# Making the mask rows of two attention layers on VectorE instead of ScalarE

## The chip, the cores and the metric

The kernel runs on one core of a Trainium2 chip. The metric is the device time of one execution, in microseconds (us). Three timed runs of the kernel before took 3186.9, 3188.81 and 3189.63 us; the median is 3188.81.

## What is computed

Eight layers work in turn on x, 128 sequences of 64 tokens with 128 features (8192 rows): four pairs of a gated cross-attention and a gated feed-forward layer. Every layer adds its result to x. The change touches the first and the last cross-attention, which have a mask over the context's 64 tokens. Cut to what matters, with scale = 64 ** -0.5:

```python
def L0_xattn(x, context, mask, W_q, W_k, W_v, W_o, b_o):   # 8 heads of 64, context 64 x 96
    q, k, v = x @ W_q, context @ W_k, context @ W_v
    sim = einsum('bhid,bhjd->bhij', q, k) * scale
    sim = where(mask[:, None, None, :], sim, max_neg)
    out = einsum('bhij,bhjd->bhid', softmax(sim), v)
    return out @ W_o + b_o

def L3_xattn(...):    # 16 heads of 64, one learned null key and value more, layer norms of x and of the result
    full_mask = pad(mask, ((0, 0), (1, 0)), constant_values=True)
    sim = where(full_mask[:, None, None, :], sim, max_neg)
```

## The kernel before

The whole of x stays on the chip as 64 tiles of 128 rows (two sequences each). The layers run one after another with a barrier between them. Each engine has its own program; order between engines comes from semaphores alone, and inside an engine from the order of its program.

`wide_attention` does the three wide cross-attentions. Layer 0 and layer 3 have `masked` set, the middle one not. The rows are worked in groups of four tiles (TG = 4, 16 groups). A `Unit` is one group and eight heads, so layer 0 has 16 units and layer 3, with 16 heads in two passes, has 32. A unit has four steps, t = 0 to 3, one tile each. The loop over units goes by twos (u = 0 and 1); its first and last passes are written out and the middle ones are a hardware loop. The counter n numbers the steps.

In step n TensorE transposes the probabilities of tile n (L777), projects the output of tile n - 1 (L709), multiplies probabilities and values (L699), makes the scores of tile n + 2 (L687), then the values of tile n + 1 and one key and one query product of a unit further on (L349 to L351). PSUM holds one set of scores (`ps_s`).

ScalarE copies results out of PSUM: the transposed probabilities (L916), the output (L925), values (L846), keys (L838) and queries (L842), and takes the exponential (`probs`, L863). GpSimd scales the probabilities (`scale_probs`, L561 and L562), splits and spreads the context and the rows (L537 to L553), adds biases (L326) and raises to powers for the norms (L321, L568).

VectorE's step has, in this order: a norm's scaling where due (L311), `sums` of tile n + 1 (a reduce L982 and a reciprocal L984), an addition to x, `shift` of tile n + 2, and moments or final norm where due. `shift` adds the mask row to the scaled scores (L964), takes the maximum (L968) and subtracts it (L976). When t == 2, `shift(n + 2)` is that of the next unit's first tile.

The mask lies on the chip as bytes, `mask`, 128 partitions by 64 tiles by 64 context tokens, one DMA per masked layer. `nm` holds, for each of two units in turn, the 128x256 fp32 rows that `shift` adds: 0 where the mask byte is 1, and -3.0e38 where it is 0. They are made by `mask_rows`, once per unit (L867), on ScalarE:

```python
def mask_rows(un):
    tiles = mask[:, bass.ds(un.g * TG, TG), :]
    A.activation(nm[un.u], tiles, ACT.Copy, bias=NEG, scale=-NEG).then_inc(nm_ready, 1)
```

For the first unit it is called in the prologue (L895), before the first queries are copied. After that it is called in step t == 0 for the next unit (L928), behind the output's copy and ahead of the values' copy, after a wait that all shifts of the unit which last used the buffer are done. VectorE waits for `nm_ready` at the first shift of a unit (L961).

Of the kernel before, what the change touches and what calls it, by code (L numbers as in the profile page):

```python
# [8 lines left out]
ALU = mybir.AluOpType  # L9
ACT = mybir.ActivationFunctionType  # L10
# [6 lines left out]
TG = 4  # L17
# [8 lines left out]
NEG = -3.0e38  # L26
# [341 lines left out]
def need(eng, sem, v):  # L368

    if not isinstance(v, int) or v > 0:  # L370
        eng.wait_ge(sem, v)
# [22 lines left out]
def wide_attention(c, d, layer, boot=None):  # L394
# [6 lines left out]
    V, A, T, G = nc.vector, nc.scalar, nc.tensor, nc.gpsimd  # L401
    null = layer == 3
    masked = layer in (0, 3)
# [6 lines left out]
    scale = DH ** -0.5  # L410
# [20 lines left out]
    if masked:  # L431
        mask = c.mask
        nm = [w([TG, S]), w([TG, S])]
# [14 lines left out]
    mask_in, cs_in, spread_ready = sem("mask_in"), sem("cs_in"), sem("spread")  # L448
# [3 lines left out]
    s_ready, s_read, max_ready, sub_ready, exp_ready = (sem(n) for n in ("s", "s_read", "max", "sub", "exp"))  # L452
# [44 lines left out]
    first = Unit(0, 0, passes)  # L497
    second = first.next()

    with nc.Block() as block:  # L500
# [333 lines left out]
        @block.scalar  # L834
        def _(act):
            def take_key(un, j, bank):
                act.wait_ge(k_full, un.k * 4 + j + 1)
                A.activation(kT[un.u][:, j, :], jobs[bank], ACT.Copy).then_inc(k_done, 1)  # L838

            def take_query(un, j, bank):  # L840
                act.wait_ge(q_full, un.k * 4 + j + 1)
                A.activation(qT[un.u][:, j, :], jobs[bank], ACT.Copy).then_inc(q_done, 1)  # L842

            def take_values(n, t, src):
                act.wait_ge(v_full, n + 1)
                A.activation(vp[t % 2].rearrange("p e j c -> p (e j c)"), src, ACT.Copy).then_inc(v_done, 1)  # L846

            def take_hT(g):
                act.wait_ge(ht_full, g + 1)
                need(act, hq_low, g)  # L850
                A.activation(hT, c.ps[:, 4, :], ACT.Copy).then_inc(ht_out, 1)

            def rows_high(g, i):
                act.wait_ge(ht_out, g + 1)
                A.activation(hh[i], hT, ACT.Copy).then_inc(hq_high, 1)

            def take_null(g):
                act.wait_ge(z_ready, g + 1)
                A.activation(s0.rearrange("p t h -> p (t h)"), c.ps[:, 2, 0:TG * 2 * HP], ACT.Copy, scale=scale).then_inc(s0_ready, 1)

            def probs(n, t):
                act.wait_ge(sub_ready, n + 1)
                A.activation(pr[t % 2], sc[t % 2], ACT.Exp, scale=1.0 if masked else scale).then_inc(exp_ready, 1)  # L863

            def mask_rows(un):
                tiles = mask[:, bass.ds(un.g * TG, TG), :]
                A.activation(nm[un.u], tiles, ACT.Copy, bias=NEG, scale=-NEG).then_inc(nm_ready, 1)  # L867

            def weights_high(dst, src, parts):
                for p in range(passes):  # L870
                    cols = slice(p * HP * DH, (p + 1) * HP * DH)
                    A.activation(dst[0:parts, cols], src[:, cols], ACT.Copy).then_inc(w_high, 1)

            if boot:
                boot.scalar(act)
                act.wait_ge(boot.wk, 16)
            weights_high(kh, wk, DC)
            if boot:
                act.wait_ge(boot.ctx, 16)
            A.activation(ch[0][0:DC, :], c.ctx01[0:DC, 0, :], ACT.Copy).then_inc(high, 1)  # L880
            if boot:
                act.wait_ge(boot.wq, 16)
            weights_high(qh, wq, P)
            if boot:
                act.wait_ge(boot.wv, 16)
            weights_high(wvh, wv, DC)
            take_key(first, 0, 0), take_key(first, 1, 1)
            take_hT(0), rows_high(0, 0)
            take_key(first, 2, 0), take_key(first, 3, 1)
            if boot:  # L890
                act.wait_ge(boot.ctx1, 16)
            A.activation(ch[1][0:DC, :], c.ctx01[0:DC, 0 if null else 1, :], ACT.Copy).then_inc(high, 1)
            if masked:
                act.wait_ge(mask_in, 16)
                mask_rows(first)  # L895
            for j in range(NJ):
                take_query(first, j, j % 2)
            if null:
                take_null(0)
            take_values(0, 0, jobs[0])  # L900
            if not null:
                take_hT(1), rows_high(1, 1)
            take_key(second, 0, 1), take_key(second, 1, 0)
            probs(0, 0)
            take_query(second, 0, 1), take_query(second, 1, 0)
            probs(1, 1)
            if boot:
                boot.scalar_gates(act)

            def body(it, last):  # L910
                for u in range(2):
                    for t in range(TG):
                        un, n = Unit(it, u, passes), it * 8 + (4 * u + t)
                        end = last and u == 1
                        act.wait_ge(pt_ready, n + 1)
                        A.activation(ptT.rearrange("p j q -> p (j q)"), c.ps[:, 4, :], ACT.Copy).then_inc(pt_out, 1)  # L916
                        if had_target(it, u, t, last):
                            take_query(*((target_of(un, t - 1) if t else
                                          (Unit(it, 0, passes).next().next(), 1) if u else (Unit(it - 1, 1, passes).next().next(), 1))),
                                       0)  # L920
                        if null and t == TG - 1 and u == 1:
                            act.wait_ge(r_ready, un.g + 1)
                            A.activation(r0T[0:2 * HP, :], c.ps[0:2 * HP, 4, :], ACT.Copy).then_inc(r0t_ready, 1)
                        act.wait_ge(o_ready, n + 1)
                        A.activation(oT.rearrange("p j b q -> p b j q"), ps_o, ACT.Copy).then_inc(ot_out, 1)  # L925
                        if masked and t == 0 and not end:
                            need(act, s_read, n)
                            mask_rows(un.next())  # L928
                        if turns(u, t, last):
                            take_hT(un.g + 1 if null else un.k + 2)  # L930
                        if not (end and t == TG - 1):
                            take_values(n + 1, t + 1, value_bank(t))
                        if turns(u, t, last) and not null:
                            rows_high(un.k + 2, u)
                        if has_target(u, t, last):
                            take_key(*target_of(un, t), 1)
                        if null and t == 0 and u == 0 and not (isinstance(it, int) and it == 0):
                            act.wait_ge(acc_ready, un.g)
                            need(act, added, un.g - 1)
                            A.activation(y.rearrange("p t c -> p (t c)"), c.ps[:, 7, :], ACT.Copy).then_inc(acc_out, 1)  # L940
                        if t < 2 or not end:
                            probs(n + 2, t)
                        if null_turns(u, t, last):
                            take_null(un.g + 1)
                        if turns(u, t, last) and null:
                            act.wait_ge(q_full, un.k * 4 + 8)
                            rows_high(un.g + 1, 0)

            by_twos(act, units // 2, body)
            if null:  # L950
                act.wait_ge(acc_ready, c.ngroup)
                act.wait_ge(added, c.ngroup - 1)
                A.activation(y.rearrange("p t c -> p (t c)"), c.ps[:, 7, :], ACT.Copy).then_inc(acc_out, 1)

        @block.vector
        def _(ve):
            def shift(n, un, t):

                if masked and t == 0:
# [76 lines left out]
            context_low(second)  # L1036
            ve.wait_ge(ht_full, 1)
            norm.scale(ve, 1)
            shift(0, first, 0)
            if null:  # L1040
                norm.take_moments(ve, 1, 1)
# [6 lines left out]
            def body(it, last):  # L1048
                for u in range(2):
                    for t in range(TG):  # L1050
                        un, n = Unit(it, u, passes), it * 8 + (4 * u + t)
                        end = last and u == 1
# [8 lines left out]
                        if not null and t == 0:  # L1061
                            if u:
                                add(it * 2)
                            elif not (isinstance(it, int) and it == 0):
                                add(it * 2 - 1)
                        if t < 2 or not end:
                            if boot and isinstance(it, int) and it == 0 and u == 0 and t == 3:
                                ve.wait_ge(s_ready, n + 3)
                                boot.vector_second(ve, c.ps[:, 3, S:S + NE0])
                            shift(n + 2, *two_on(un, t))  # L1070
# [1635 lines left out]
```

## Time and profile before

| | |
|---|---|
| median of three runs | 3188.81 us (3186.9 to 3189.63) |
| the profiled execution's own time | 3188.81 us |
| its span | 3187.0 us |
| TensorE busy (matmul) | 2977.2 us, 93% |
| VectorE busy | 2235.7 us, 70% |
| ScalarE busy | 1576.0 us, 49% |
| GpSimd busy | 1201.5 us, 38% |

Layer 0 covers the span's first 345 us or so, layer 3's attention about 2372 to 3100. Busy shares over the whole span mix eight layers with different limits, so stretches inside the two masked layers have to be read by themselves. The profile names engines PE (TensorE matmul), PEld (its weight loads), DVE (VectorE), ACT (ScalarE) and POOL (GpSimd).

### The profile page before, as it was taken

How to read it: one execution, taken by the hardware profiler on the slowest of the kernel's cores; microseconds unless marked ns; L12 is line 12 of the kernel's file. 1: busy time of each engine (PE TensorE's matmuls, PEld its weight loads, DVE VectorE, ACT ScalarE, POOL GpSimd, SP SyncE). 2: the span in 40 equal slices, each digit the busy share in tenths (PEclk: the TensorE clock that was granted, in tenths of full speed). 3: DMA queues.
4: the chain of work that ended last, by engine and by line, in shares of the span. 5: the costliest groups of instructions: out<-in, count | busy, mean ns of one | idle time of the engine just before them, and what ended most of it. 6: DMA issues, size and time to landing. Idle time of an engine off the chain costs nothing. (4 is left out here: it accounts for less than half of the span.)

```text
span 3187.0 us, 91077 instructions
## 1 busy us (share of the span) xinstructions
PE 2977.2 (93%) x35250; PEld 2312.9 (73%) x35250; DVE 2235.7 (70%) x6007; ACT 1576.0 (49%) x2929; POOL 1201.5 (38%) x1402
## 2 busy tenths in 40 slices
PE   8999799999998999779997999999989999999978
PEld 6888445555556888656776888888877888888864
DVE  7777566566655666667877877777767777777755
ACT  6777212111114777456663333333336776777746
POOL 6676200000004777544430000000015676676653
PEclk9999899999998999979998999999999999999989
DMA  6000166665651000011102332333320000000001
GB/s 164 10 10 8 60 190 182 179 179 163 163 167 33 11 10 8 2 57 25 27 16 89 102 97 97 101 107 107 104 67 10 11 10 7 10 10 9 8 2 54
DMA packets 111032, 212.22 MB, mean 67 GB/s; under 512 B 18769, under 2 KB 30609, under 8 KB 110353
## 3 DMA queue, kind: packets, MB, share of 16 engines
q1 hardware_dynamic: 110352, 209.19, 22.6%
q8 instruction: 91, 1.49, 0.2%
q10 hardware_dynamic: 512, 0.92, 0.1%
q14 instruction: 77, 0.62, 0.1%
HBM read 198.50 MB, written 5.77 MB: 64 GB/s over the span
## 5 line engine op out<-in xcount | busy, mean ns | idle before, releaser
L349 PE MATMUL ps<-parts 128*128 128x512 f32 (+2 forms) x1568 | 623.9, 398 | 29.9 <-DVE parts L1014 18.4
L350 PE MATMUL ps<-parts 128*128 128x512 f32 (+2 forms) x1568 | 565.3, 361 | 0.0
L351 PE MATMUL ps<-parts 128*128 128x512 f32 (+2 forms) x1568 | 564.8, 360 | 0.0
L319 POOL TENSOR_TENSOR rstd<-mv,eps 128x4 f32<-128x4 f32 x112 | 23.3, 208 | 1224.3 <-DVE mv L302 1224.1
L1934 ACT ACTIVATE work<-ps 128x512 f32<-128x512 f32 x272 | 162.6, 598 | 453.8 <-PE ps L351 453.6
L349 PEld LDWEIGHTS ps<-parts 128*128 128x128 f32 (+1 forms) x1568 | 299.3, 191 | 101.0 <-ACT work L846 25.8
L351 PEld LDWEIGHTS ps<-parts 128*128 128x128 f32 (+1 forms) x1568 | 298.8, 191 | 47.2
L350 PEld LDWEIGHTS ps<-parts 128*128 128x128 f32 (+1 forms) x1568 | 301.0, 192 | 20.8
L562 POOL TENSOR_TENSOR work<-work 128x512 f32<-128x512 f32 x256 | 267.0, 1043 | 127.9 <-DVE work L984 127.9
L1900 PEld LDWEIGHTS ps<-early,work 128*128 128x128 f32 x2176 | 281.6, 191 | 30.3 <-DVE work L1991 11.4
L1900 PE MATMUL ps<-early,work 128*128 128x128 f32 x2176 | 289.4, 276 | 8.2 <-DVE x L2098 8.1
L1981 DVE TENSOR_TENSOR work<-work,ps 128x512 f32<-128x512 f32 x272 | 185.8, 683 | 132.0 <-PE ps L1900 124.0
L2257 PE MATMUL ps<-work,early 128*128 128x512 f32 x512 | 249.9, 611 | 11.5 <-DVE work L2509 11.5
L982 DVE TENSOR_REDUCE work<-work 128x8 f32<-128x512 f32 (+1 forms) x256 | 174.0, 679 | 122.7 <-ACT work L863 121.2
L964 DVE SCALAR_TENSOR_TENSOR ps<-ps,work 128x512 f32<-128x512 f32 x192 | 134.2, 699 | 158.1 <-PE ps L687 157.6
L846 ACT ACTIVATE work<-ps 128x512 f32<-128x512 f32 x256 | 153.1, 598 | 160.3 <-PE ps L351 157.1
L925 ACT ACTIVATE work<-ps 128x512 f32<-128x512 f32 x256 | 153.0, 598 | 128.7 <-PE ps L699 127.6
L968 DVE TENSOR_REDUCE work<-ps 128x8 f32<-128x512 f32 x256 | 176.9, 691 | 53.9 <-PE ps L687 47.3
L699 PE MATMUL ps<-work 64*64 64x64 f32 x8192 | 179.5, 225 | 18.5 <-ACT work L916 17.0
L1991 DVE TENSOR_TENSOR work<-work 128x512 f32<-128x512 f32 x256 | 177.2, 692 | 17.9 <-DVE work L1981 4.3
L699 PEld LDWEIGHTS ps<-work 64*64 64x64 f32 x8192 | 146.8, 135 | 55.3 <-issue 36.9
L2509 DVE TENSOR_TENSOR work<-work 128x1024 f32<-128x1024 f32 x128 | 154.5, 1218 | 41.0 <-DMA work<-gate_rows 36.7
(297 smaller groups left out, 6256.2 us busy)
## 6 DMA issues: line engine op xcount, KB each, us to landing
work<-gate_rows SPq DMA_DIRECT2D x128, 512.0 KB, 5.1
work<-expert_rows SPq DMA_DIRECT2D x512, 128.0 KB, 2.9
work<-gate_rows SPq DMA_DIRECT2D x128, 256.0 KB, 7.7
work<-in_ctxT SPq DMA_DIRECT2D x72, 192.0 KB, 2.4
out<-x SPq DMA_DIRECT2D x16, 256.0 KB, 2.3
work<-work SPq DMA_DIRECT2D x224, 16.0 KB
work<-work SPq DMA_DIRECT2D x16, 128.0 KB, 3.5
early<-in_l0f_w SPq DMA_DIRECT2D x1, 1536.0 KB, 8.3
```

The source lines that it names most:

```text
L349: T.matmul(out, lh, rh, start=True, stop=False)
L350: T.matmul(out, lh, rl, start=False, stop=False)
L351: return T.matmul(out, ll, rh, start=False, stop=True)
L562: G.tensor_tensor(pn[t % 2], pr[t % 2][:, :, 0:S], bc(rec[t % 2], 2, S), ALU.mult).then_inc(p_ready, 1)
L699: last = T.matmul(ps_o[e * DH:e * DH + DH, b, j, :], vp[t % 2][rows, e, j, :], ptT[rows, j, b * S:b * S + S], start=True, stop=True)
L968: V.tensor_reduce(mx[t % 2], ps_s, AX.X, ALU.max).then_inc(max_ready, 1)
L982: V.tensor_reduce(den[t % 2], pr[t % 2], AX.X, ALU.add).then_inc(sum_ready, 1)
L1900: last = T.matmul(acc[:, t * D:(t + 1) * D], aT[b][:, t * P:(t + 1) * P], c.w["l2f_d"][:, j, :], start=(j == 0 and t == 0), stop=(j == NB ...
L1934: A.activation(sg[b], ps_g[b], ACT.Silu).then_inc(silu_ready, 1)
L1981: out = V.tensor_tensor(aT[b], sg[b], ps_u[b], ALU.mult)
L1991: V.tensor_tensor(aT[b], aT[b], wb[j % WR], ALU.mult).then_inc(a_ready, 1)
L2257: T.matmul(ps_q[u], c.w["l0f_w"][:, at:at + P], hw[p % NHW][:, e, :], start=(p == 0 and e == 0), stop=(p == NP - 1 and e == 1))
```

## The change

`mask_rows` moves from ScalarE's program to VectorE's and becomes a tensor_scalar, (mask - 1) * 3.0e38, with the same values. The first unit's call moves to VectorE's prologue, between the second norm's scaling and the first shift, with the wait for the mask's DMA. The others move from step t == 0 to step t == 2, between `sums` and the `shift` that is the first to read the new rows. The wait on `s_read` that stood in front of them on ScalarE is gone. Semaphore `nm_ready` and VectorE's wait on it stay.

```diff
@@ scalar
-            def mask_rows(un):
-                tiles = mask[:, bass.ds(un.g * TG, TG), :]
-                A.activation(nm[un.u], tiles, ACT.Copy, bias=NEG, scale=-NEG).then_inc(nm_ready, 1)
...
-            if masked:
-                act.wait_ge(mask_in, 16)
-                mask_rows(first)
             for j in range(NJ):
                 take_query(first, j, j % 2)
...
                         A.activation(oT.rearrange("p j b q -> p b j q"), ps_o, ACT.Copy).then_inc(ot_out, 1)
-                        if masked and t == 0 and not end:
-                            need(act, s_read, n)
-                            mask_rows(un.next())
@@ vector
+            def mask_rows(un):
+                tiles = mask[:, bass.ds(un.g * TG, TG), :]
+                V.tensor_scalar(nm[un.u], tiles, 1.0, -NEG, ALU.subtract, ALU.mult).then_inc(nm_ready, 1)
...
             norm.scale(ve, 1)
+            if masked:
+                ve.wait_ge(mask_in, 16)
+                mask_rows(first)
             shift(0, first, 0)
...
                         if t < 2 or not end:
+                            if t == 2 and masked:
+                                mask_rows(un.next())
                             if boot and isinstance(it, int) and it == 0 and u == 0 and t == 3:
...
                             shift(n + 2, *two_on(un, t))
```

## Rows read from the trace of the kernel before

**Rows 1.** The page's first line.
```profile
span 3187.0 us, 91077 instructions
```

**Rows 2.** Stretches of layers 0 and 3: busy us, granted clock, DMA share, GB/s.
```profile
core 0: us, PE busy (x) PEld busy (x) DVE busy (x) ACT busy (x) POOL busy (x), PEclk, DMA share, GB/s
160.00:240.00 80.00, 80.00 (x1454) 70.37 (x1457) 61.38 (x141) 60.82 (x111) 57.22 (x57) 1.00 0.04 10
2660.00:2740.00 80.00, 78.01 (x1396) 67.05 (x1395) 62.51 (x182) 56.03 (x103) 56.40 (x71) 1.00 0.03 10
```

**Rows 3.** Line L867: min, median, max ns, first and last start.
```profile
L867 ACT ACTIVATE work<-mask x48: 403/408/408, 15.6 to 3050.4; 128x256 f32 x40, 128x256 f32<-128x256 uint8 x8
```

**Rows 4.** Timeline of ScalarE, a layer 0 step t == 0: start, us, instruction, idle.
```profile
177.21 0.41 ACT L867 ACTIVATE work<-mask 128x256 f32 x1
178.06 0.60 ACT L846 ACTIVATE work<-ps 128x512 f32<-128x512 f32 x1 [0.44 <-PE ps L351]
```

**Rows 5.** Timeline, the prologues of layer 0 and layer 3.
```profile
15.31 0.39 PE L351 MATMUL ps<-parts 128*128 128x512 f32 x1
...
15.59 0.40 ACT L867 ACTIVATE work<-mask 128x256 f32<-128x256 uint8 x1
...
15.90 0.58 ACT L842 ACTIVATE work<-ps 128x512 f32<-128x512 f32 x1
15.92 1.63 POOL L552 TENSOR_TENSOR parts<-parts,zero 96x512 fp32r<-96x512 f32 x1
...
2388.69 0.50 PE L349 MATMUL ps<-parts 128*128 128x512 f32 x1 [0.19 <-ACT early L842]
```

**Rows 6.** Lines L2002 and L338, VectorE instructions with one input in SBUF.
```profile
L2002 DVE TENSOR_SCALAR work<-work x16: 218/221/222, 1690.0 to 2301.9; 128x128 f32<-128x128 f32 x16
...
L338 DVE CAST parts<-work x16: 418/420/422, 1689.0 to 2299.5; 128x512 fp32r<-128x512 f32 x16
```

**Rows 7.** Timelines of VectorE and of GpSimd, a layer 0 step t == 2.
```profile
146.70 0.20 DVE L984 RECIPROCAL work<-work 128x8 f32<-128x8 f32 x1
147.97 0.70 DVE L964 SCALAR_TENSOR_TENSOR ps<-ps,work 128x512 f32<-128x512 f32 x1 [1.06 <-PE ps L687]
...
146.26 1.28 POOL L552 TENSOR_TENSOR parts<-parts,zero 96x512 fp32r<-96x512 f32 x1
147.50 0.73 POOL L553 TENSOR_TENSOR parts<-parts,zero 96x256 fp32r<-96x256 f32 x1
```

**Rows 8.** Timelines of VectorE and of GpSimd, a layer 3 step t == 2.
```profile
2716.36 0.20 DVE L984 RECIPROCAL work<-work 128x8 f32<-128x8 f32 x1
2717.82 0.70 DVE L964 SCALAR_TENSOR_TENSOR ps<-ps,work 128x512 f32<-128x512 f32 x1 [1.25 <-PE ps L687]
...
2717.10 1.28 POOL L544 TENSOR_TENSOR parts<-work,parts 128x512 fp32r<-128x512 f32 x1
...
2718.50 1.04 POOL L562 TENSOR_TENSOR work<-work 128x512 f32<-128x512 f32 x1
```

**Rows 9.** Timelines of VectorE and of GpSimd, the first norm's scaling.
```profile
8.32 1.29 DVE L311 TENSOR_SCALAR work<-x,mv,rstd 128x128 f32<-128x128 f32 x1 [0.31 <-POOL rstd L321]
...
8.26 1.27 POOL L552 TENSOR_TENSOR parts<-parts,zero 96x512 fp32r<-96x512 f32 x1
9.49 0.73 POOL L553 TENSOR_TENSOR parts<-parts,zero 96x256 fp32r<-96x256 f32 x1
```

**Rows 10.** Timeline behind the shift of rows 8.
```profile
2719.67 0.59 PEld L777 LDWEIGHTS ps<-ident,work 128*128 128x128 f32 x4
...
2720.27 0.64 ACT L863 ACTIVATE work<-work 128x520 f32<-128x520 f32 x1 [0.27 <-DVE work L976]
...
2720.81 0.58 ACT L916 ACTIVATE work<-ps 128x512 f32<-128x512 f32 x1
...
2721.54 0.29 PE L699 MATMUL ps<-work 64*64 64x64 f32 x4
```

**Rows 11.** Timeline of layer 0's first pass, around its step t == 2.
```profile
43.89 0.69 DVE L964 SCALAR_TENSOR_TENSOR ps<-ps,work 128x512 f32<-128x512 f32 x1
...
47.33 0.29 PE L699 MATMUL ps<-work 64*64 64x64 f32 x4 [0.62 <-ACT work L916]
```

## The prediction

> **What bounds the kernel now.** The profiled execution is the median one of the three timed runs (3188.81 us), so the sum is made against 3188.81 directly; its span is 3187.0 us [rows 1], and the 1.8 us around it don't change. A measurement of this kernel tells a time from no change if it moves by about 0.2%, that is 6.4 us.
>
> I read the stretches first. In the masked layer 0 TensorE is busy in all of 80 us; in layer 3, the other masked one, in 78.01 of 80. The granted clock is 1.00 (2.4 GHz) in both. VectorE has 61 to 63 of 80, ScalarE 56 to 61 [rows 2]. So layer 0 is bound by TensorE outright, and layer 3 but for about half a microsecond in each 20. Work taken off ScalarE or put on VectorE counts only where it ends a wait of TensorE. The other layers don't run this code.
>
> Then I read what is moved, and the order of time around the old and the new place.
>
> **What the change removes.** 48 ScalarE instructions of 0.408 us, 19.6 us of ScalarE work [rows 3]. In the steady steps ScalarE goes from this instruction to copying the next values out of PSUM, and there it sits idle 0.44 us until TensorE's product is done [rows 4]. Without the mask instruction it would sit idle 0.85 us. The layer 3 units look the same (0.45). Worth: nothing, 46 times. ScalarE's wait on `s_read` before it goes too; it held nothing.
>
> In each prologue the instruction stands in front of `take_query`. In layer 0 the first query product ends at 15.31 + 0.39 = 15.70, ScalarE starts to copy it at 15.90, so the mask held it 0.2 us at most; in layer 3 the same place shows TensorE idle for 0.19 us on that copy [rows 5]. Gain: 0.14 us (my reading of TensorE's hole in layer 0, bounded by 0 and 0.2) plus 0.19 us, about 0.3 us in all.
>
> **What it adds.** 48 tensor_scalar instructions on VectorE, 128x256, bytes in and fp32 out. The trace has no such shape on VectorE. The nearest rows: a tensor_scalar with immediates on 128x128 takes 221 ns, a cast of 128x512 takes 420 ns [rows 6]. A line through the two gives 221 + 199/3 = 0.29 us at 256 columns. The other end is 0.42 us, what the cast takes for twice the columns, should bytes run at half the rate of fp32. I take 0.29; it is a like operation. In all 14 to 20 us of VectorE work, on an engine with 17 to 19 us idle in every 80.
>
> **Where it lies.** The new call is in step t == 2, between `sums` (reduce, reciprocal) and `shift` for the first step of the next unit, the only step that reads the fresh rows. In layer 0 the reciprocal ends at 146.70 + 0.20 = 146.90 and the shift's first instruction starts at 147.97, after 1.06 us of waiting for TensorE's scores [rows 7]. In layer 3 the reciprocal ends at 2716.56 and the shift starts at 2717.82, with 1.25 us of the same wait [rows 8]. I went through all 46 such places: 44 have 1 us or more, the last unit of layer 3 has 0.6, and one has none (below). So 0.29 or 0.42 us fits, by length alone. Behind the new instruction are queued the shift, the norm's moments and the next `sums`; exponentials on ScalarE and the probabilities' scaling on GpSimd wait for those.
>
> Length is not all. At 146.90 GpSimd is inside L552 (146.26 to 147.54), followed without a gap by L553 [rows 7]. What that does to a tensor_scalar stands in the first norm: the first L311 starts at 8.32, takes 1.29 us and ends at 9.61, just 0.08 us after GpSimd's L552 (8.26 + 1.27 = 9.53), while L553 is already recorded from 9.49 [rows 9]. So a VectorE tensor_scalar waits for the end of the running GpSimd instruction, then gets in before the next one. The new instruction, twice as many columns, should then end 0.15 us behind L552 (0.08 plus 0.07 for 128 more columns at the slope above), 0.28 us at half rate: 147.69 to 147.82, still ahead of 147.97. In layer 3 the running instruction ends where L544 begins, 2717.10, so the new one ends by 2717.4, 0.4 us ahead [rows 8]. The other half of the layer 3 units has a wider gap and only a 0.2 us instruction next on GpSimd. Cost in the steady steps: 0.
>
> The cover is thin in one sense: if the shift does come late, ScalarE's exponential comes late (it already waits 0.27 us for L976), then the copy L916 behind it, which ends at 2721.39, and TensorE's L699 starts at 2721.54 [rows 10]. So only 0.15 us of lateness is free; beyond that it goes to TensorE.
>
> The exception is the first pass of layer 0: the shift at 43.89 starts without idle time, because VectorE is late there, and TensorE later waits 0.62 us on the chain that starts there [rows 11]. The new instruction costs its length: 0.29 us, 0.42 at the other end. The prologue copies of it lie on VectorE between the norm's scale and a shift that waits about 1 us for scores; the mask has landed by then, since ScalarE used it at 15.59 [rows 5]. Cost 0.
>
> The Trainium skill (SBUF — State Buffer, the section on SBUF's two separate sides) says that VectorE in a two-port mode and GpSimd exclude each other for a whole instruction, whichever starts first, and VectorE: DVE Perf Modes (what auto-detection checks) puts a one-source SBUF-to-SBUF operation in such a mode. The trace agrees for the wait of L311; that bytes count as such a source no run here shows. By that rule GpSimd would also wait for the new instruction, which is rival 1, and the sum would be about 3190 us.
>
> **Sum.** 3188.81 − 0.14 − 0.19 + 0.29 + 0 = 3188.8 us.
>
> **Rivals.**
> Rival 1, GpSimd is held up in its turn. A two-input VectorE instruction did this at 15.92: L552 took 1.63 us there, 1.28 us in the steady step [rows 5, 7]. For it in layer 3: L562 ends at 2718.50 + 1.04 = 2719.54, and TensorE loads its result at 2719.67 [rows 8, 10], 0.13 us of slack. Against it: L553 behind L311 took its usual 0.73 us [rows 7, 9]. If L544 starts 0.15 to 0.28 us late, TensorE loses 0.02 to 0.15 us in each of some 15 units, 0.3 to 2.3 us: about 3190 us. Layer 0 has far more slack there. Still no measurable change.
>
> Rival 2, slower: the new instruction does not get in between two GpSimd instructions and waits for the second as well. In layer 0 it would end at 147.50 + 0.73 + 0.15 = 148.38, 0.41 us late, less the 0.15 that is free: 0.26 us in some 13 units, 3.4 us. In layer 3 at 2717.10 + 1.28 + 0.15 = 2718.53, 0.71 us late, 0.56 us net in 15 units, 8.4 us; the other layer 3 units lose nothing. Sum 11.8: 3200.6 us. It decides from a lateness of about 0.3 us in all units. Against it stands that L311 got in ahead of L553; for it, that the new instruction is twice as long and waits longer.
>
> Rival 3, slower still: VectorE's length counts in every unit, 48 times 0.29 to 0.42 us, 14 to 20 us, 3203 to 3209 us. It needs the gaps of [rows 7, 8] to be no real idle time; TensorE's 80 of 80 speaks against it.
>
> Rival 4, faster: ScalarE's relief reaches TensorE. The most it can bring is 19.6 us, 3169 us; it needs 0.13 us a unit to show. The 0.44 us of idle behind the instruction speaks against it [rows 4].
>
> **How the numbers follow.** No change 0.66, rival 1 0.14, rival 2 0.11, rival 3 0.03, rival 4 0.06. So within 0.2%: 0.80; slower 0.14; faster 0.06. The likeliest is 3188.8. For the range: downward the prologue gains (0.4 at most), the spread of the runs shown (1.9 below the median), and an allowance of 2 us, mine and carried by no row, for the two engines' programs being laid out anew; upward the same spread (0.8) and allowance, 0.13 for the length at its other end and rival 1's 2.3 us: 3184.5 to 3194. Rivals 2, 3 and 4 lie beyond and are left out, 0.20 together.
>
> **What would show it.** In the profile after: the new instruction 48 times on VectorE; alone 0.29 us long (0.42 tells the other end), in steady units recorded at 0.7 to 0.8 us because it waits for GpSimd; the shift behind it still released by TensorE's L687, with the idle time now short. ScalarE's idle before L846 grows from 0.44 to about 0.85 in steps t == 0. TensorE stays at 80 of 80 and 78 of 80, and units keep their length. The prediction is wrong if the shift's releaser becomes VectorE or GpSimd, if L916 comes later relative to L699, or if L777 is released by GpSimd in layer 3.

## The result and the profile after

The changed kernel takes 3207.65 us (median of four runs, 3204.94 to 3210.41) against 3188.3 us (3186.9 to 3189.63) for the kernel before: ratio 1.006, interval 1.0046 to 1.0074. It is slower by 19.35 us, three times what can be told from no change, and lies outside the predicted range. The profiled execution took 3206.64 us, its span against [rows 1] grew by 17.3 us. One of e8_order's ten runs (4206.86 us) and two of the kernel before beside it (4748.21 and 15935.71 us) were in a slow state, which the kernel before shows as well, and are left out of its numbers below.

The windows that answer to [rows 2], after; columns as there:

```profile
span 3204.3 us, 91068 instructions
...
core 0: us, PE busy (x) PEld busy (x) DVE busy (x) ACT busy (x) POOL busy (x), PEclk, DMA share, GB/s
160.00:240.00 80.00, 75.05 (x1344) 65.75 (x1342) 66.34 (x128) 54.56 (x99) 53.38 (x52) 1.00 0.04 10
2660.00:2740.00 80.00, 78.10 (x1397) 66.97 (x1395) 61.84 (x176) 55.16 (x99) 54.72 (x69) 1.00 0.03 10
```

TensorE was busy 80.00 of 80 us in layer 0 and is now busy 75.05; in layer 3 nothing moved (78.01 to 78.10). So the loss is one of layer 0. Laid out by unit (four steps, from the starts of the shifts of the same step), a steady unit of layer 0 (one away from the ends of the layer, where the times repeat) took 19.58 or 19.77 us before and takes 21.15 or 21.32 after; the 11 units from the fourth on take 233.18 us in place of 216.46, 16.7 more. The first three units are the same in sum (69.11 and 69.0). Layer 3's steady units keep 20.98 to 21.0 and 21.95 us, and TensorE's stretch in its attention is 710.64 us against 710.89.

VectorE and then GpSimd of the changed kernel around a layer 0 step t == 2, which answer to [rows 7] (the shift is L958 now, the mask instruction L949):

```profile
149.74 0.20 DVE L978 RECIPROCAL work<-work 128x8 f32<-128x8 f32 x1
149.89 2.54 DVE L949 TENSOR_SCALAR work<-mask 128x256 f32 x1
152.62 0.70 DVE L958 SCALAR_TENSOR_TENSOR ps<-ps,work 128x512 f32<-128x512 f32 x1 [0.19 <-DVE work L949]
```

```profile
149.29 1.28 POOL L552 TENSOR_TENSOR parts<-parts,zero 96x512 fp32r<-96x512 f32 x1
150.53 0.74 POOL L553 TENSOR_TENSOR parts<-parts,zero 96x256 fp32r<-96x256 f32 x1
151.22 1.05 POOL L562 TENSOR_TENSOR work<-work 128x512 f32<-128x512 f32 x1
152.22 1.36 POOL L326 TENSOR_TENSOR x<-x,rows 128x512 f32 x1
```

These rows hold the cause of the 16.7 us. The mask instruction is recorded for 2.54 us. It arrives 0.6 us into L552, and ends at 152.43, 0.16 us after the end of L562 (151.22 + 1.05 = 152.27). Three GpSimd instructions in a row, L552, L553 and L562, have gone by, and it gets in ahead of the fourth, L326, which takes 1.36 us where it took 1.30 in the same step of before:

```profile
149.19 1.30 POOL L326 TENSOR_TENSOR x<-x,rows 128x512 f32 x1
```

The shift starts 152.62 − 149.94 = 2.68 us behind the reciprocal's end; in [rows 7] it was 147.97 − 146.90 = 1.07. It is 1.61 us late.

What the lateness costs, from the timelines of ScalarE and TensorE of the changed kernel behind that shift:

```profile
154.81 0.63 ACT L863 ACTIVATE work<-work 128x512 f32<-128x512 f32 x1 [1.63 <-DVE work L970]
155.34 0.58 ACT L909 ACTIVATE work<-ps 128x512 f32<-128x512 f32 x1
```

```profile
156.07 0.69 PE L699 MATMUL ps<-work 64*64 64x64 f32 x32 [1.50 <-ACT work L909]
```

The exponential L863 waits for the shift's last instruction, the copy L909 (L916 before) is queued behind the exponential, and TensorE's L699 waits 1.50 us for the copy. The chain is the one of [rows 10], now with a hole at its end. In the list of waits of the window from 80 to 340 us, by waiter and releaser (us in total, times, longest), it stands as follows, after and then before:

```profile
PE ps L699 <- ACT work L909: 17.7, 12, 1.7
```

```profile
PE ps L699 <- ACT work L916: 1.0, 3, 0.4
```

That is 17.7 us of TensorE idle time in 12 waits, where it was 1.0 us in 3 waits.

In layer 3, VectorE and GpSimd of the changed kernel, an even unit:

```profile
2732.11 0.20 DVE L978 RECIPROCAL work<-work 128x8 f32<-128x8 f32 x1
2732.24 0.29 DVE L949 TENSOR_SCALAR work<-mask 128x256 f32 x1
2733.56 0.70 DVE L958 SCALAR_TENSOR_TENSOR ps<-ps,work 128x512 f32<-128x512 f32 x1 [1.03 <-PE ps L687]
```

```profile
2731.85 1.02 POOL L568 TENSOR_TENSOR work<-work,half 128x4 f32<-128x4 f32 x1
2732.84 1.28 POOL L544 TENSOR_TENSOR parts<-work,parts 128x512 fp32r<-128x512 f32 x1
```

The mask instruction runs 0.29 us in the middle of GpSimd's L568, a power on four elements per partition, and isn't blocked by it. The shift still waits for TensorE. In the odd units it runs in the same way inside L321, another such power.

One unit of layer 3 is different, the second (VectorE, then GpSimd):

```profile
2431.36 1.14 DVE L949 TENSOR_SCALAR work<-mask 128x256 f32<-128x256 uint8 x1
```

```profile
2431.07 1.27 POOL L544 TENSOR_TENSOR parts<-work,parts 128x512 fp32r<-128x512 f32 x1 [2.01 <-ACT parts L855]
2432.31 0.25 POOL L561 TENSOR_TENSOR work<-work 128x8 f32<-128x8 f32 x1
2432.53 1.04 POOL L562 TENSOR_TENSOR work<-work 128x512 f32<-128x512 f32 x1
```

Here the mask instruction comes 0.29 us into L544, waits for its end (2432.34) and ends at 2432.50, although L561 and L562 follow L544 without a gap. It isn't passed over, as the prediction had it for all units, and the shift isn't late: it starts at 2432.91, 1.47 us behind the reciprocal, where it was 1.50 before.

### The profile page after: what moved, and what is told of

Its sections match the earlier page's. It is cut to its first block and busy times, and to the rows that moved or that the text cites. A ratio compares the mean times of both kernels' runs of the same rounds, so it can differ in the third digit from the quotient of the medians.

```text
span 3204.3 us, 91068 instructions
## 1 busy us (share of the span) xinstructions
PE 2975.4 (93%) x35250; PEld 2311.5 (72%) x35250; DVE 2276.8 (71%) x6055; ACT 1560.0 (49%) x2881; POOL 1202.2 (38%) x1402
## 3 DMA queue, kind: packets, MB, share of 16 engines
q8 instruction: 90, 1.47, 0.2%
## 5 line engine op out<-in xcount | busy, mean ns | idle before, releaser
L562 POOL TENSOR_TENSOR work<-work 128x512 f32<-128x512 f32 x256 | 266.8, 1042 | 130.3 <-DVE work L978 130.3
L958 DVE SCALAR_TENSOR_TENSOR ps<-ps,work 128x512 f32<-128x512 f32 x192 | 134.2, 699 | 133.6 <-PE ps L687 124.6
L699 PE MATMUL ps<-work 64*64 64x64 f32 x8192 | 179.5, 225 | 39.2 <-ACT work L909 37.7
L699 PEld LDWEIGHTS ps<-work 64*64 64x64 f32 x8192 | 147.3, 135 | 76.4 <-issue 59.5
L863 ACT ACTIVATE work<-work 128x512 f32<-128x512 f32 (+1 forms) x256 | 161.6, 631 | 64.8 <-DVE work L970 63.8
```

The lines of the kernel that those rows point to most:

```text
L562: G.tensor_tensor(pn[t % 2], pr[t % 2][:, :, 0:S], bc(rec[t % 2], 2, S), ALU.mult).then_inc(p_ready, 1)
L699: last = T.matmul(ps_o[e * DH:e * DH + DH, b, j, :], vp[t % 2][rows, e, j, :], ptT[rows, j, b * S:b * S + S], start=True, stop=True)
```

## The experiments

The questions: is it the exclusion of the two engines, or something in the instruction itself (its mask bytes, its length, its scalars); is ScalarE's relief really worth nothing; and by what rule does GpSimd pass a waiting VectorE instruction over. In layer 0 a steady unit of 19.58 or 19.77 us means no loss, 21.15 us or more the full one. All diffs are against the changed kernel but that of e5_none.

**e1_pointer.** One of the two scalars comes from memory. (The first call also waits for the constants to be made, in the prologue, here and in e3_fp32.)

```
-    V.tensor_scalar(nm[un.u], tiles, 1.0, -NEG, ALU.subtract, ALU.mult)
+    V.tensor_scalar(nm[un.u], tiles, c.w["ones"][:, 0:1], -NEG, ALU.subtract, ALU.mult)
```

> The changed kernel, but the 1.0 that is subtracted comes from a column of ones (one value per partition) instead of a constant. Theory: whether a waiting VectorE instruction gets in between two GpSimd instructions depends on the kind of its scalars; the norm's L311 and L244, which got in after the first, have such columns, the mask instruction had constants. Then it gets in behind L552: about 0.85 us recorded in layer 0's steady units instead of 2.55, units of 19.6 to 19.8 us instead of 21.15 to 21.3, time about 3189 us. Rivals (its 256 columns, or its byte source, keep it out): still 2.55 us, units of 21.2, about 3207 us.

Measured: 3209.5 us, ratio 1.0069 (1.0052 to 1.0086), steady units 21.15 and 21.2. VectorE's timeline in the place of the rows above:

```profile
150.86 2.55 DVE L949 TENSOR_SCALAR work<-mask,ones 128x256 f32 x1
```

The same 2.55 us. The kind of scalar isn't the cause.

**e2_four.** Four instructions of 128x64 in place of one of 128x256.

```
+    for i in range(TG):
+        last = V.tensor_scalar(nm[un.u][:, i, :], mask[:, bass.ds(un.g * TG + i, 1), :][:, 0, :],
+                               1.0, -NEG, ALU.subtract, ALU.mult)
+    last.then_inc(nm_ready, 1)
```

> The changed kernel, but the mask rows are made by four instructions of 128x64 instead of one of 128x256, constants and bytes as before. Theory of length: a short instruction gets in between two GpSimd instructions, so the first ends about 0.05 us behind L552 and the second behind L553; each later one waits for one more GpSimd instruction, and the fourth ends after L326: the shift comes later still, about 1.3 us more per unit, some 3225 us. Theory of scalars or of the byte source: the first of the four waits 2.5 us as the one did, and the other three follow at once or wait for L326 as well: 3207 to 3225 us. What tells them apart is the recorded length of the first: 0.75 us against 2.5 us.

Measured: 3254.92 us in one run (3188.28 before), steady units of 24.05 to 25.57 us. VectorE, then GpSimd:

```profile
139.55 3.89 DVE L950 TENSOR_SCALAR work<-mask 128x64 f32 x4
143.63 0.70 DVE L960 SCALAR_TENSOR_TENSOR ps<-ps,work 128x512 f32<-128x512 f32 x1 [0.19 <-DVE work L950]
```

```profile
138.97 1.27 POOL L552 TENSOR_TENSOR parts<-parts,zero 96x512 fp32r<-96x512 f32 x1
140.21 0.72 POOL L553 TENSOR_TENSOR parts<-parts,zero 96x256 fp32r<-96x256 f32 x1
140.89 1.04 POOL L562 TENSOR_TENSOR work<-work 128x512 f32<-128x512 f32 x1
141.90 1.29 POOL L326 TENSOR_TENSOR x<-x,rows 128x512 f32 x1
```

The first piece, a quarter as long, takes 2.46 us of these 3.89 and ends behind L562 all the same; the second takes 1.31 us, because it waits for L326 in addition; the last two find GpSimd idle and take 0.18 us each. Length isn't the cause, and a second instruction of this kind bought a wait of its own.

**e3_fp32.** The source is a tile of 256 fp32 zeros in place of the mask bytes, and no mask is applied.

```
-    V.tensor_scalar(nm[un.u], tiles, 1.0, -NEG, ALU.subtract, ALU.mult)
+    tiles = c.zero[:, 0:TG * S].rearrange("p (t k) -> p t k", k=S)
+    V.tensor_scalar(nm[un.u], tiles, 1.0, 0.0, ALU.subtract, ALU.mult)
```

> The changed kernel, but the instruction reads 256 fp32 zeros instead of the mask's bytes and multiplies by 0, so no mask is applied in layers 0 and 3; constants, columns and place are the same. Theory of the byte source: with fp32 in it gets in behind L552, 0.85 us recorded, units of 19.6 to 19.8 us, about 3189 us. Rivals (scalars, length): 2.55 us recorded and about 3207 us. Alone it should take 0.29 us either way.

Measured: 3206.1 us in one run (3188.28 before). The row is the same but for its source and 0.03 us:

```profile
149.88 2.58 DVE L950 TENSOR_SCALAR work<-zero 128x256 f32<-128x256 f32 x1
```

The bytes aren't the cause.

**e4_step1.** In layer 0 the instruction goes behind the shift of step t == 1, where GpSimd is idle; layer 3 stays as changed.

```
-                            if t == 2 and masked:
+                            if t == 2 and null:
                                 mask_rows(un.next())
...
                             shift(n + 2, *two_on(un, t))
+                            if t == 1 and layer == 0 and not end:
+                                mask_rows(un.next())
```

> The changed kernel, but in layer 0 the mask instruction stands behind the shift of step t == 1 instead of ahead of the shift of step t == 2; layer 3 as in the changed kernel. GpSimd has nothing to do there for about 1.6 us. Theory (the loss is the wait for GpSimd at that place, in front of the shift): the instruction takes its own 0.29 us, units are 19.6 to 19.8 us again, time within 3 us of the kernel before. Rival (VectorE's added work or ScalarE's missing instruction lengthens the unit wherever it stands): units stay at 21.2 us, about 3207 us.

Measured over ten runs: 3188.51 us against 3188.28, ratio 1.0002 (0.9992 to 1.0012); steady units 19.58 and 19.78. VectorE, GpSimd and the window:

```profile
143.44 0.28 DVE L949 TENSOR_SCALAR work<-mask 128x256 f32 x1
144.79 0.69 DVE L976 TENSOR_REDUCE work<-work 128x8 f32<-128x512 f32 x1 [1.07 <-ACT work L863]
```

```profile
143.83 1.28 POOL L544 TENSOR_TENSOR parts<-work,parts 128x512 fp32r<-128x512 f32 x1 [1.59 <-ACT parts L855]
```

```profile
160.00:240.00 80.00, 80.00 (x1493) 70.45 (x1484) 61.85 (x143) 58.98 (x106) 57.54 (x57) 1.00 0.04 12
```

The same instruction, in an idle stretch of both engines, takes its own 0.28 us and delays nobody; the whole loss is gone. So the loss is a matter of the place. In the first pass the new place isn't idle:

```profile
38.24 1.30 DVE L949 TENSOR_SCALAR work<-mask 128x256 f32<-128x256 uint8 x1
```

```profile
38.11 1.27 POOL L544 TENSOR_TENSOR parts<-work,parts 128x512 fp32r<-128x512 f32 x1 [0.71 <-ACT parts L855]
39.34 1.33 POOL L552 TENSOR_TENSOR parts<-parts,zero 96x512 fp32r<-96x512 f32 x1
40.63 0.73 POOL L553 TENSOR_TENSOR parts<-parts,zero 96x256 fp32r<-96x256 f32 x1
```

There it waits for L544 and ends at 39.54, ahead of L552.

**e5_none** (diff against the kernel before). ScalarE makes mask rows for the first two units of a layer and none after; most units then use rows that aren't their own.

```
-                mask_rows(first)
+                mask_rows(first), mask_rows(second)
...
-                            need(act, s_read, n)
-                            mask_rows(un.next())
+                            pass
...
-                if masked and t == 0:
-                    ve.wait_ge(nm_ready, un.k + 1)
+                if masked and isinstance(n, int) and n == 0:
+                    ve.wait_ge(nm_ready, 2)
```

> The kernel before without its per-unit mask instruction on any engine: the two buffers are filled once in the prologue of each masked layer, on ScalarE, and used for all units, so the mask of most units is not their own. It prices what ScalarE's relief is worth. Theory (nothing, ScalarE waits for TensorE behind it): within 3 us of the kernel before. Rival (the relief is worth something and the changed kernel gave it back): up to 19 us faster, 3170 us.

Measured over ten runs: 3187.55 us against 3187.56, ratio 1.0003 (0.9993 to 1.0012), with ScalarE's 403 ns instruction 4 times in place of the 48 of [rows 3]. The relief alone is worth nothing that can be told within 0.1%, so there was no gain for the new wait to eat.

**e6_reduce.** A reduction over an axis of one element, same bytes in and same tile out, same place; it doesn't apply the mask.

```
-    V.tensor_scalar(nm[un.u], tiles, 1.0, -NEG, ALU.subtract, ALU.mult)
+    V.tensor_reduce(nm[un.u], bc(tiles, 3, 1), AX.X, ALU.max)
```

> The changed kernel with the mask instruction in its place, but made as a tensor_reduce over an axis of length 1, so that the mask bytes are copied as 0.0 and 1.0 and no -3.0e38 is applied. Reduces of SBUF data (L982 in the kernel before) run beside GpSimd's instructions without growing longer. Theory (the loss is an exclusion between GpSimd's instructions and a two-port tensor_scalar, not the place and not the length): the instruction takes about 0.35 to 0.42 us in every unit, layer 0's units are 19.6 to 19.8 us again, time within 3 us of the kernel before. Rival (anything in front of this shift costs): units of 20 us and more.

Measured: 3188.15 us against 3187.56, ratio 0.9999 (0.999 to 1.0009), steady units 19.58 and 19.77. VectorE, then GpSimd:

```profile
145.45 0.42 DVE L949 TENSOR_REDUCE work<-mask 128x256 f32 x1
146.56 0.70 DVE L958 SCALAR_TENSOR_TENSOR ps<-ps,work 128x512 f32<-128x512 f32 x1 [0.70 <-PE ps L687]
```

```profile
144.87 1.27 POOL L552 TENSOR_TENSOR parts<-parts,zero 96x512 fp32r<-96x512 f32 x1
```

Here VectorE's instruction starts 0.58 us into L552 as well, and runs through beside it: 0.42 us, and the shift waits for TensorE again. Same place, source and neighbours, another form: no loss. This and e4_step1 show the cause, the exclusion between this form on VectorE and GpSimd's large instructions.

**e7_mid.** Is the pass-over a matter of the phase at which the instruction arrives? VectorE waits for the end of L552 first.

```
-    G.tensor_tensor(dst[un.u][0:DC, :, 0:2, :], st, zero, ALU.add)
+    G.tensor_tensor(dst[un.u][0:DC, :, 0:2, :], st, zero, ALU.add).then_inc(half_spread, 1)
...
                             if t == 2 and masked:
+                                if layer == 0:
+                                    ve.wait_ge(half_spread, un.k * 2 + 4)
                                 mask_rows(un.next())
```

> The changed kernel, but in layer 0's steps t == 2 VectorE waits for the end of GpSimd's L552 before it issues the mask instruction, so that it comes to GpSimd's port just as L553 starts, not 0.6 us into L552. Theory of phase (an instruction that comes within about 0.1 us of a GpSimd instruction's start, as all those did that got in behind the first, is let in behind that one; a later one is passed over): it gets in behind L553, recorded about 0.8 us, 1.0 us earlier than in the changed kernel, units of about 20.2 us, time about 3195 us. Theory of queue order (GpSimd's instructions that are already handed over go first): L562 is handed over long before, so it still gets in only behind L562, units of 21.2 us, 3207 us.

Measured: 3204.73 us against 3187.56, ratio 1.005 (1.0032 to 1.0068), units 21.15 and 21.20. VectorE, then GpSimd (whose lines are numbered one higher here, L554 for L553 and L563 for L562):

```profile
148.92 1.68 DVE L950 TENSOR_SCALAR work<-mask 128x256 f32 x1 [0.81 <-POOL parts L553]
```

```profile
148.70 0.72 POOL L554 TENSOR_TENSOR parts<-parts,zero 96x256 fp32r<-96x256 f32 x1
149.38 1.04 POOL L563 TENSOR_TENSOR work<-work 128x512 f32<-128x512 f32 x1
```

It arrives later, in another instruction, and still ends behind the third. In these units it comes 0.22 us after L553's start (L554 here), outside the 0.1 us of the theory, so they don't test it. Three units at the ends of the layer do, where it came 0.08 us after that start and was recorded at 3.05, 1.82 and 1.82 us (the second of them at 296.95, L553 at 296.87): it was passed over by L562 all the same. And the second unit of layer 3, shown above, came 0.29 us after a start and got in behind that one. My theory of the phase falls.

**e8_order.** GpSimd holds L562 back until the mask rows are there, in layer 0.

```
+                        if t == 2 and layer == 0 and not end:
+                            pool.wait_ge(nm_ready, un.k + 2)
                         if not (end and t == TG - 1):
                             scale_probs(n + 1, *one_on(un, t))
```

> The changed kernel, but in layer 0's steps t == 2 GpSimd waits for the mask rows before it issues L562. VectorE's program is that of the changed kernel. Theory of queue order (a VectorE instruction waits for those GpSimd instructions that were handed over before it, and those alone): L552 and L553 were, L562 now is not, so the mask instruction gets in behind L553, recorded about 1.55 us instead of 2.55. The shift is then 0.5 to 0.6 us late instead of 1.6, and of that about 0.15 us is free: units about 0.4 to 0.5 us longer than before (20.0 to 20.2 us), time 3193 to 3196 us. Rival (the length of the wait has another cause, such as a retry after a fixed time): still 2.5 us recorded and units of 21.2 us or more, 3207 us.

Measured over nine runs: 3188.75 us against 3186.76 (eleven runs), ratio 1.0013 (1.0002 to 1.0023), steady units 19.58 and 19.77. VectorE, then GpSimd:

```profile
143.68 0.83 DVE L951 TENSOR_SCALAR work<-mask 128x256 f32 x1
144.79 0.70 DVE L960 SCALAR_TENSOR_TENSOR ps<-ps,work 128x512 f32<-128x512 f32 x1 [0.28 <-PE ps L689]
```

```profile
143.08 1.28 POOL L552 TENSOR_TENSOR parts<-parts,zero 96x512 fp32r<-96x512 f32 x1
144.31 0.78 POOL L553 TENSOR_TENSOR parts<-parts,zero 96x256 fp32r<-96x256 f32 x1
```

I had expected it to get in behind L553. It gets in behind L552 already, and L553 takes 0.78 in place of 0.73 us. This is nearly what my prediction had said of the changed kernel: 0.83 us recorded (it had 0.7 to 0.8), the shift on time. So whether the gap between L552 and L553 is open to VectorE hangs on what stands behind L553 in GpSimd's queue. The steady units are as before, so the 2.0 us between the medians have no place there; where they lie isn't shown, and they are within 0.2%.

**e9_split.** e8_order, with L553 of layer 0 (layer 3 keeps the old line) split into two halves that are both ready.

```
-    G.tensor_tensor(dst[un.u][0:DC, :, 2, :], st[:, :, 0, :], zero[:, :, 0, :], ALU.add)
+    G.tensor_tensor(dst[un.u][0:DC, 0:2, 2, :], st[:, 0:2, 0, :], zero[:, 0:2, 0, :], ALU.add)
+    G.tensor_tensor(dst[un.u][0:DC, 2:4, 2, :], st[:, 2:4, 0, :], zero[:, 2:4, 0, :], ALU.add)
```

> The kernel of the run before this one (GpSimd issues L562 only once the mask rows are made), with layer 0's L553 split into two instructions of half its rows, so that two GpSimd instructions stand ready behind L552 when the mask instruction comes, neither of them L562. Theory of number (the port stays with GpSimd while two or more of its instructions stand ready, and goes to VectorE when one does): the mask instruction is passed over, recorded 1.3 us or more, and ends behind the first or the second half. Rival (it is L562, released by the same reciprocal as the mask instruction, that takes the port with it): it still gets in behind L552, recorded 0.85 us.

Measured: 3192.92 us in one run (3190.89 before). VectorE, then GpSimd (the halves are L554 and L555):

```profile
145.10 0.84 DVE L955 TENSOR_SCALAR work<-mask 128x256 f32 x1
```

```profile
144.52 1.27 POOL L552 TENSOR_TENSOR parts<-parts,zero 96x512 fp32r<-96x512 f32 x1
145.75 0.50 POOL L554 TENSOR_TENSOR parts<-parts,zero 96x128 fp32r<-96x128 f32 x1
```

Two ready instructions behind L552 don't close the gap: it still gets in behind L552. The bare number of ready GpSimd instructions isn't the rule; the second unit of layer 3, with L561 and L562 behind L544, says the same.

**e10_bias.** L326, the instruction behind L562, goes to step t == 3 in layer 0, from the second pass of the loop on.

```
-                        if t == 2 and not null and not last:
+                        if t == (3 if layer == 0 and prior else 2) and not null and not last:
                             norm.bias(pool, un.k + 2)
```

> The changed kernel, but in layer 0's loop passes from the second on the bias addition L326 moves from step t == 2 to the end of step t == 3, so that nothing stands ready behind L562. Theory of number, judged at the end of each GpSimd instruction: at the end of L552 two stand ready (L553, L562), at the end of L553 only L562, so the mask instruction gets in behind L553: recorded about 1.55 us, 0.5 us of lateness left, units of about 20.0 to 20.3 us, some 3195 us. Theory that the order is fixed when the mask instruction comes: it still waits for L562, 2.5 us recorded, units of 21.2 us, 3207 us.

Measured: 3195.15 us in one run (3190.89 before), units 20.14 and 20.29, 0.54 more than before. VectorE, then GpSimd:

```profile
147.13 1.52 DVE L949 TENSOR_SCALAR work<-mask 128x256 f32 x1
148.85 0.70 DVE L958 SCALAR_TENSOR_TENSOR ps<-ps,work 128x512 f32<-128x512 f32 x1 [0.19 <-DVE work L949]
```

```profile
146.55 1.28 POOL L552 TENSOR_TENSOR parts<-parts,zero 96x512 fp32r<-96x512 f32 x1
147.78 0.73 POOL L553 TENSOR_TENSOR parts<-parts,zero 96x256 fp32r<-96x256 f32 x1
148.47 1.09 POOL L562 TENSOR_TENSOR work<-work 128x512 f32<-128x512 f32 x1
```

With one instruction fewer behind it, it gets in one gap earlier, behind L553, and the loss per unit falls to a third. It is also a third point on the price. The shift comes 148.85 − 147.19 (the reciprocal's end, 146.99 + 0.20) = 1.66 us behind the reciprocal, 0.59 late, and a unit is 0.54 longer. In the changed kernel it is 1.61 late for 1.56, in e8_order 144.79 − 143.73 = 1.06, not late, for 0. At these three points lateness of the shift goes to TensorE one for one, less 0.05 us. It doesn't stay so: in e2_four the shift is 143.63 − 139.62 (the reciprocal's end) = 4.01 us behind the reciprocal, 2.94 late, and units are over 4 us longer.

## Why the prediction was wrong

**The step that failed** is "So a VectorE tensor_scalar waits for the end of the running GpSimd instruction, then gets in before the next one". The first half holds for GpSimd's large instructions: L552 blocks it, as e1_pointer to e3_fp32 show for either kind of scalar, length and source, and e6_reduce by its contrast. It doesn't hold in layer 3, where the running instruction of [rows 8] is the power L568: there the instruction took its own 0.29 us and waited for nobody. The second half was drawn from one kind of place, the first norm's L311 [rows 9], and doesn't hold in layer 0's steady units: L553 and L562 went by, and the instruction was recorded at 2.54 us, not 0.7 to 0.8. Two of the signs that the prediction had named for itself came true there: the shift's releaser is VectorE's L949, and L909 (L916 before) comes so late that L699 waits for it. The term "cost in the steady steps: 0" came out at 1.56 us in a layer 0 unit, 16.7 us in the 11 units from the fourth on. That two GpSimd instructions pass a waiting one is visible in no row of before; what was there to be used was the length of GpSimd's unbroken run at that moment, four instructions from L552 to L326. I had looked only as far as the next.

**Rival 2 had the mechanism, and the wrong places and size.** It let the instruction wait for one more GpSimd instruction and gave 0.41 us of lateness in layer 0; it waited for two more, 1.61 us. In layer 3 it expected 0.71 us in some 15 units and there was none, because the GpSimd instruction that runs there is a small power that doesn't block, so that the mask instruction is done before L544 starts; the one unit where L544 did run, the second, shows it getting in right behind it. Its 3200.6 us is a sum of one part too small and one part that didn't happen. Its chance of 0.11 rested on L311 alone and was too small: a single kind of situation can't carry a rule about who is served first.

**Rival 1** holds in its sign only: the GpSimd instruction behind the mask instruction is held up by 0.06 us (L326, 1.36 for 1.30) and by 0.05 in e8_order (L553, 0.78 for 0.73); nobody waits for it.

**Rival 3** gives a time near the measured one (3203 to 3209 us) for a reason that is refuted: e4_step1 and e6_reduce add the same or more VectorE time in all 48 places and lose nothing.

**Rival 4** falls with e5_none: ScalarE's relief is worth nothing within 0.1%.

**What was right.** The length alone: 0.24 to 0.29 us wherever nothing blocks it, not 0.42. The prologues: the first shift stands 11.55 us behind TensorE's first instruction of layer 0 in place of 11.64, and 15.76 in place of 15.94 in layer 3, so 0.09 and 0.18 us against 0.14 and 0.19. Layer 3 unchanged in time. The chain from the shift by L863 and the copy to L699 is the one that carries the loss, and the free lateness is 0.05 us in layer 0, not the 0.15 read in layer 3. The first pass costs nothing in sum for another reason than predicted: its second unit grows by 2.70 us (the mask instruction waits 3.76 us there), and the third shrinks by as much, where before TensorE stood idle for 2.29 us and now has no such hole; why isn't shown. The first three units together take anything from 65.96 us (e5_none) to 69.11 (before) in the runs without a loss, so their sum prices nothing under 3 us.

The sum with what was measured: 3188.81 (the profiled execution) − 0.27 for the prologues + 16.7 in layer 0 = 3205.2, against 3206.64 in the profiled execution after. The remaining 1.4 us are less than the spread of the runs, 5.5 us.

**What stays open** is the rule by which GpSimd's next instruction or the waiting one is served. Holding L562 back opens the gap between L552 and L553, taking L326 away opens that between L553 and L562. The phase of the arrival (e7_mid) and the bare number of ready instructions (e9_split) don't decide. The time that GpSimd has been given ahead doesn't by itself either, as far as the rows go: in e10_bias the gap behind L552 was closed with L553 and L562 to come, 0.73 + 1.09 = 1.82 us, while in the first pass of e4_step1 the gap behind L544 was open with L552 and L553 to come, 1.33 + 0.73 = 2.06 us. The second unit of layer 0 in the changed kernel is a place where even L326 passed it, 3.76 us in all, with another power (L226) next. No run here puts these into one rule.

The Trainium skill (SBUF — State Buffer, the section on the two separate sides) has the shared port as an exclusive lock for the whole instruction, held by whichever starts first. The rows above agree as to the block by L552. They don't agree for the powers: L568 had started first, and the mask instruction ran its 0.29 us beside it. And the one that waited was not the next to be served: it was passed over twice.

No version beats the kernel before. e4_step1 is as fast, and e5_none, which leaves the work out, shows that there is nothing to be gained from it.

## What to carry to other kernels

Before a one-source VectorE instruction in SBUF (a tensor_scalar here) is put in a place, look at GpSimd at that moment, and price it, at the worst, at the end of GpSimd's unbroken run (the third of its four instructions here, the last of them in one unit), not at the end of the instruction that is running; to be safe, what hides it must be longer than that. If it must lie there, a stretch where GpSimd is idle (e4_step1), a form that isn't blocked, where one does the work (the reduction of e6_reduce doesn't apply the mask), or a wait in GpSimd's queue behind it (e8_order) takes the cost away. And when a rule of who is served first comes from one kind of place in a trace, give its opposite a real chance.

## What the runs showed of the hardware

- A waiting VectorE instruction was passed over by two GpSimd instructions that started after it had arrived; the record of 2.54 us is wait, all but 0.29. In the second unit of layer 3 it was not: it got in right behind L544, with L561 and L562 to follow (1.14 us).
- A GpSimd power on 128x4 (L568, 1.02 us) didn't block a VectorE tensor_scalar (0.29 us beside it), while GpSimd's L552 on 96x512 did.
- A reduction over an axis of one element, on the same bytes, took 0.42 us and wasn't blocked by L552; the tensor_scalar, 0.29 us alone, was.
- Whether the instruction gets in between two GpSimd instructions changed with what stood one or two places further behind (0.83, 1.52 and 2.54 us for the same instruction in the same place).
